# Splitting two float32 projections of the second attention into float32r parts, with in-place scans in a ring of three, batched small steps and a new order on every engine

## The chip, the cores and the metric

One NeuronCore of a Trainium2 chip runs the whole program. The metric is the device time of one execution in microseconds (us). The kernel before takes 1335.6 us (median of three runs, 1335.15 to 1338.34).

## What is computed

64 sequences of 128 tokens by 256 features (`x`) and as many of a context (`c`) go through four stages, all in float32 accuracy:

```
x1 = LN(attn16(relu(x Wq+bq), relu(c Wk+bk), relu(c Wv+bv), query mask) + x)   # 16 heads of 16
u  = rms(x1) @ in_proj; xBC = silu(causal_conv4(u)); dt = softplus(u_dt + bias)
y  = scan over 128 tokens: h = h*exp(dt*A) + dt*xh (x) B ; y = h.C + D*xh      # 8 heads of 64, state 128
h  = x1 + rms(y * silu(z)) @ out_proj
out = h + softmax((LN(h) Wq1)(c Wk1)^T / sqrt(32)) (c Wv1) @ Wo                # 8 heads of 32
```

The change is in the last line (the projections `Wq1` and `Wo`), in how the scan's decay tile is held, and in the order of everything.

## The kernel before, in words

The 64 sequences are worked on in 32 groups (`NG`) of two (`NB`), 256 tokens each. A group passes 25 kinds of step on TensorE (PE), 28 on VectorE (DVE), 29 on ScalarE (ACT), 15 on GpSimd (POOL) and 8 on the SyncE queue (SP). Each step is a small function of the group number `g` and a part; what an engine does is its list of calls, written out by hand: a prologue, a loop `for g in range(NG - 9)` in which the calls belong to up to six different groups, and an epilogue. All hand-offs are semaphores; every step waits for a count and raises one. An engine never leaves its list's order, so a step that waits holds all that stand behind it.

PSUM is eight banks. Which step writes which bank, and in which cyclic order, is the table `USES` (L21): an entry is (step, part, lag in groups) and its bank. `bank()` gives a step its bank and the semaphore of the step that used it last (`freed`), which must have been read out.

The steps that matter here, on PE:

- `proj3` (L315 to L321) multiplies in float32r with both operands split in a high and a low part: three matmuls (low x high, high x low, high x high) for each of the two halves of K=256. `q`, `k`, `k1`, `cp` (six parts) and `z` use it, `v`, `v1` and `o` have the same three products written out.
- `full` (L562 to L565), used by `q1`, and `wp` (L658 to L670) multiply in plain float32: two matmuls of 256 columns for a product where `proj3` has six. The trace shows each float32 matmul as two records.
- `sA`, `sT` and `sC` compute scores with 32-row pieces of the array, `av` and `oC` write 32-column pieces, `y` 64-column pieces. `tn`, `ot`, `nt`, `bd`, `bx`, `ht` and `tC` are transposes; `gm` and `dp` are small products.

On DVE: `mA` and `mC` are maxima of the scores, `tap` (18 a group) the convolution, `dc` (12 a group) the softplus polynomial, `scan` the decay products (L977, from `DB` into `L`), `lg` their product with `gm` (L986), `hm` (L1048) the mean term of the last LayerNorm, `fin` the last residual add, `nl` (L883) the low part of a split read from PSUM. On ACT, `he` copies the transposed LayerNorm output into `HT`, `oT` the attention output into `OT`. On POOL, `rs`, `nr` and `hr` raise variances to the power -1/2, one sequence at a time.

The decay goes through DRAM: `dk` (DVE) writes `decT`, `dec_out` (SP) stores it, `dec_in` (SP) loads it back broadcast to 128 partitions into `DB[b]`, and `scan` reads it. The two tiles `DB` are free again once the scan has read them.

The six stages overlap as follows in one turn of the loop: while PE does `cp(g+5)`, it also does `q(g+7)`, `sA(g+6)`, `y(g+4)`, `sC(g+3)` and `wp(g+2)`.

Of the kernel before, what the change touches and what calls it, by code (L numbers as in the profile page):

```python
# [5 lines left out]
F32 = mybir.dt.float32  # L6
# [30 lines left out]
def program(nc, a):  # L37
    with ExitStack() as ctx:
# [22 lines left out]
        wq1 = sb("wq1", [128, 2, 256])  # L61
        wo = sb("wo", [128, 2, 256])
# [33 lines left out]
        PTA = ring("PTA", 4, [128, 4, 128])  # L96
# [6 lines left out]
        sta = ring("sta", 4, [128, 48])  # L103
        stb = ring("stb", 4, [128, 16])
        stn = ring("stn", 4, [128, 1])
# [11 lines left out]
        DB = ring("DB", 2, [128, 1024])  # L117
        L = sb("L", [128, 8, 128])
        XH = sb("XH", [128, 512])
# [6 lines left out]
        HT = sb("HT", [128, 2, T])  # L126
# [89 lines left out]
        def sync(e):  # L216
# [97 lines left out]
        def tensor(e):  # L314
# [252 lines left out]
            def q1(g, m):  # L567
                if ok(g):
# [8 lines left out]
                    if m == 0:  # L577
                        e.wait_ge(s_h, 2 * g + 2)
# [1477 lines left out]
```

## Time and profile before

| | |
|---|---|
| median of 3 runs | 1335.6 us (1335.15 to 1338.34) |
| span of the profiled execution | 1337.2 us, 43414 instructions |
| the profiled execution's own time | no other number for it is given than the span, which lies inside the range of the runs, 1.6 us above their median |
| PE / PE weight loads / DVE / ACT / POOL busy | 1291.6 / 1148.0 / 1208.1 / 1130.8 / 928.7 us |
| granted TensorE clock | full (1.00) in the middle, 0.99 on average |
| DMA | 87.0 MB, 65 GB/s on average |

Busy time is the time in which an engine had an instruction in it. Durations of neighbouring instructions on one engine overlap a little in the records (by about 0.08 us on DVE), so the distance from one start to the next is what an instruction takes up of the engine. In the chain of waits ("the chain of work that ended last") each piece begins where the one before it ended, so its lengths do add up.

### The profile page before, as it was taken

Reading aid. Unit: us, or ns where it says so; the run is one execution under the profiler, and the core shown is the slowest. Engines: PE = TensorE matmul, PEld = TensorE weight load, DVE = VectorE, ACT = ScalarE, POOL = GpSimd, SP = SyncE. Lnnn points to the kernel's source line nnn. Section 1 sums busy time; section 2 is a strip of 40 time slices with the busy share of each in tenths; the row PEclk is TensorE's granted clock in tenths of the full one; section 3 lists DMA queues with packets and bytes.
Section 4 is the critical chain, followed back from the end, with each engine's and each line's share of the span. In section 5 each row is a group of like instructions: output and inputs, shape, how many; then the busy total and the mean of one; then the engine's idle time right before and its main releaser. Section 6 shows DMA issues by size and latency. Waiting matters only on the chain.

```text
span 1337.2 us, 43414 instructions
## 1 busy us (share of the span) xinstructions
PE 1291.6 (97%) x15624; PEld 1148.0 (86%) x15624; DVE 1208.1 (90%) x3056; ACT 1130.8 (85%) x3407; POOL 928.7 (69%) x1200
## 2 busy tenths in 40 slices
PE   5879999999999999999999999999999999999987
PEld 4668889988888998889998889989888898888875
DVE  6789999999999999999999999999999989999982
ACT  5658989888889988888988888998888898888875
POOL 3366777777767777777777776777777777766774
PEclk9889999999999999999999999999999999999999
DMA  6102221212221112222121222211222221111110
GB/s 203 40 34 72 69 77 38 70 56 69 77 77 62 52 49 69 77 77 77 38 66 60 69 77 77 61 53 50 69 77 77 71 71 34 62 56 57 49 57 25
DMA packets 41283, 87.00 MB, mean 65 GB/s; under 512 B 5744, under 2 KB 10992, under 8 KB 41072
## 3 DMA queue, kind: packets, MB, share of 16 engines
q1 hardware_dynamic: 40208, 83.81, 19.7%
q8 instruction: 127, 2.08, 0.6%
q14 instruction: 84, 0.69, 0.2%
q10 hardware_dynamic: 864, 0.42, 0.1%
HBM read 75.53 MB, written 8.68 MB: 63 GB/s over the span
## 4 chain that ended last, share of the span: by engine, by line
PE 87%; DVE 4%; ACT 4%; issue 2%; DMA 1%; POOL 1%; SPq 1%; ACTq 0%; DVEq 0%
PE bank L319 26%; PE bank L422 10%; PE bank L550 6%; PE bank L412 5%; PE bank L379 5%; PE bank L533 5%; PE bank L436 4%; PE bank L564 4%; PE bank L669 4%; PE bank L360 3%; PE bank L604 3%; PE bank L625 2%; PE bank L654 2%; PE bank L470 2%; PE bank L416 1%
## 5 line engine op out<-in xcount | busy, mean ns | idle before, releaser
L951 DVE SCALAR_TENSOR_TENSOR ACC<-bank,cw,ACC 128x250 f32<-128x250 f32 (+2 forms) x576 | 264.1, 462 | 5.9 <-ACT ACC L1535 3.3
L319 PE MATMUL bank<-xnT,wnl 128*128 128x256 f32 x640 | 201.6, 315 | 3.3 <-DVE xnL L883 2.3
L1622 ACT ACTIVATE PC<-bank,stc 128x128 f32<-128x128 f32 x512 | 182.5, 389 | 7.7 <-DVE stc L1068 4.3
L319 PE MATMUL bank<-xnL,wnh 128*128 128x256 f32 x640 | 180.3, 282 | 0.0
L319 PE MATMUL bank<-xnT,wnh 128*128 128x256 f32 x640 | 179.8, 281 | 0.0
L800 DVE TENSOR_REDUCE sta<-bank 128x4 f32<-128x512 f32 x256 | 163.7, 673 | 7.8 <-PE bank L379 7.5
L977 DVE TENSOR_TENSOR_SCAN L<-DB,id 128x1024 f32<-128x1024 f32 x64 | 146.8, 2293 | 0.8 <-DMA DB<-dec_scratch 0.8
L319 PEld LDWEIGHTS bank<-xnT,wnl 128*128 128x128 f32 x640 | 121.9, 190 | 26.0 <-issue 17.6
L1437 ACT ACTIVATE PTA<-bank 128x512 f32<-128x512 f32 x256 | 133.3, 628 | 9.0 <-PE bank L416 5.3
L1916 POOL TENSOR_TENSOR PC<-PC,stc 128x512 f32<-128x512 f32 x128 | 132.1, 1042 | 11.3 <-DVE stc L1075 11.3
L319 PEld LDWEIGHTS bank<-xnL,wnh 128*128 128x128 f32 x640 | 122.4, 191 | 0.0
L319 PEld LDWEIGHTS bank<-xnT,wnh 128*128 128x128 f32 x640 | 121.6, 190 | 0.0
L1871 POOL TENSOR_TENSOR XH<-XH,dtt 128x512 f32<-128x512 f32 x64 | 80.6, 1260 | 56.6 <-ACT XH L1552 56.5
L1622 ACT ACTIVATION_READ_ACCUMULATOR PC<-bank,stc 128x1 f32 x512 | 117.4, 229 | 0.0
L1535 ACT ACTIVATE ACC<-bank,cw 128x256 f32<-128x256 f32 x192 | 109.7, 573 | 8.3 <-PE bank L319 8.2
L1807 POOL TENSOR_TENSOR cL<-cT,cH 128x512 fp32r<-128x512 f32 x31 | 55.8, 1799 | 77.7 <-ACT cH L1372 77.7
L1880 POOL TENSOR_TENSOR Y<-Y,SZ 128x512 f32<-128x512 f32 x64 | 85.8, 1341 | 21.6 <-DVE Y L1011 18.9
L1886 POOL TENSOR_TENSOR Yl<-Y,Yh 128x512 fp32r<-128x512 f32 x64 | 82.6, 1291 | 20.0 <-ACT Yh L1580 19.9
L1423 ACT ACTIVATE NT<-bank,sel 128x128 fp32r<-128x128 f32 x256 | 73.4, 379 | 25.3 <-PE bank L392 25.3
L1636 ACT ACTIVATE PTC<-bank 128x512 f32<-128x512 f32 x128 | 78.6, 620 | 16.6 <-PE bank L422 16.3
L1068 DVE TENSOR_REDUCE stc<-bank 128x4 f32<-128x512 f32 x128 | 84.7, 683 | 7.5 <-PE bank L629 7.5
L1543 ACT ACTIVATE bank<-ACC 128x256 f32<-128x256 f32 x192 | 79.3, 415 | 8.5 <-DVE ACC L951 7.8
(210 smaller groups left out, 4709.9 us busy)
## 6 DMA issues: line engine op xcount, KB each, us to landing
DB<-dec_scratch SPq DMA_DIRECT2D x64, 512.0 KB, 4.0
cT<-in_cT SPq DMA_DIRECT2D x64, 256.0 KB, 2.6
xT<-in_xT SPq DMA_DIRECT2D x32, 256.0 KB, 4.0
xt<-in_xt SPq DMA_DIRECT2D x32, 256.0 KB, 3.8
out_x<-X SPq DMA_DIRECT2D x32, 256.0 KB, 4.0
QM<-qm_rows SPq DMA_DIRECT2D x32, 128.0 KB, 4.1
XC<-in_win SPq DMA_DIRECT2D x2, 644.0 KB, 6.7
PTC<-in_wout SPq DMA_DIRECT2D x2, 256.0 KB, 6.6
```

The source lines that it names most:

```text
L319: mm = e.matmul(t[:, c0:c0 + T], wt[:, k, m:m + 128], x[:, k, :], start=(n == 0), stop=(n == 5))
L422: mm = e.transpose(t[:, c0 + i * 128:c0 + (i + 1) * 128], src(i), ident[:, :])
L800: e.tensor_reduce(sta[ns % 4][:, 4 * j:4 * j + 4], t[:, :].rearrange("p (i k) -> p i k", i=4), AX_X, ALU.max, negate=True).then_inc(s_mA, 1)
L951: e.scalar_tensor_tensor(out=w, in0=t[:, 0:T].rearrange("p (b t) -> p b t", b=NB)[:, :, 0:125 + k], scalar=cw[:, c, k:k + 1], in1=w, op0=A ...
L977: e.tensor_tensor_scan(L[:, :, :].rearrange("p h t -> p (h t)"), DB[b][:, :], id8[:, :, :].rearrange("p h t -> p (h t)"), 0.0, ALU.mult, A ...
L1068: e.tensor_reduce(stc[g % 4][:, 4 * i:4 * i + 4], t[:, :].rearrange("p (i k) -> p i k", i=4), AX_X, ALU.max, negate=True).then_inc(s_mC, 1)
L1437: e.activation(PTA[n % 4][:, :, :], t[:, :].rearrange("p (i k) -> p i k", i=4), ACT.Exp).then_inc(s_eA, 1)
L1535: e.activation(ACC[n % 3][:, :, :], t[:, 0:T].rearrange("p (b t) -> p b t", b=NB), ACT.Identity, bias=cw[:, c, 4:5], scale=cw[:, c, 3:4]). ...
L1622: op = e.activation(PC[n % 4][:, p, :], t[:, p * 128:(p + 1) * 128], ACT.Exp, bias=stc[g % 4][:, 4 * i + p:4 * i + p + 1], accum_out=stc[g ...
L1880: e.tensor_tensor(cv(Y[:, :]), cv(Y[:, :]), SZ[:, :, b * 128:(b + 1) * 128], ALU.mult).then_inc(s_ga, 1)
L1886: e.tensor_tensor(Yl[:, :], Y[:, :], Yh[:, :].bitcast(F32), ALU.subtract).then_inc(s_yl, 1)
L1916: e.tensor_tensor(PC[n % 4][:, :, :], PC[n % 4][:, :, :], stc[g % 4][:, 16 + 4 * i:20 + 4 * i].unsqueeze(2).to_broadcast([128, 4, 128]), A ...
```

## The change

1. **Two projections in float32r.** `q1` and `wp` use three float32r matmuls for each float32 one. Their weights are split at the start (`wq1h`/`wq1l`, `woh`/`wol`). Their inputs need a low part as well, so `he` now writes `HTh` and a new DVE step `hl` (two a group, 128x256, PSUM and SBUF in) writes `HTl`; `oT` writes `OTh` and a new DVE step `ol` (one a group, 128x512) writes `OTl`. The banks `ht` and `oC` are freed by the new steps.
2. **Scan in place.** `L` is gone. `scan` and `lg` write into the tile they read, `DB`, now a ring of three over the 64 sequences. `dec_in` waits until `y` of three sequences before has read the tile.
3. **Buffers.** `XH` is a ring of two instead of one tile, `PTA` a ring of six instead of four; `sta`, `stb`, `stn` are views of tiles that hold both sequences of a group.
4. **Batched steps.** `rs`, `nr`, `hr` on POOL and `hm` on DVE run once for a group on 128x2 values instead of twice on 128x1.
5. **Order.** Prologues and epilogues are gone; each engine has one loop over `g` from -5 (SP from -6) to `NG - 1`, and `if ok(g)` in each step leaves out what doesn't exist. The order in the loop and the table `USES` are new.
6. `dynamic_dma_scratch_size=1024` is given to the program's constructor.

```diff
-        wq1 = sb("wq1", [128, 2, 256])
-        wo = sb("wo", [128, 2, 256])
+        wq1h, wq1l = (sb(n, [128, 2, 256], F32R) for n in ("wq1h", "wq1l"))
+        woh, wol = (sb(n, [128, 2, 256], F32R) for n in ("woh", "wol"))
-        PTA = ring("PTA", 4, [128, 4, 128])
+        PTA = ring("PTA", 6, [128, 4, 128])
-        DB = ring("DB", 2, [128, 1024])
-        L = sb("L", [128, 8, 128])
-        XH = sb("XH", [128, 512])
+        DB = ring("DB", 3, [128, 1024])
+        XH = ring("XH", 2, [128, 512])
...
             def dec_in(g, b):
-                    if ns >= 2:
-                        e.wait_ge(s_l, ns - 1)
-                    e.dma_start(DB[b][:, :], scratch[g, b * 1024:(b + 1) * 1024].rearrange(
+                    if ns >= 3:
+                        e.wait_ge(s_y, ns - 2)
+                    e.dma_start(DB[ns % 3][:, :], scratch[g, b * 1024:(b + 1) * 1024].rearrange(
...
             def q1(g, m):
-                        e.wait_ge(s_h, 2 * g + 2)
-                    full(t, 0, wq1, m, HT).then_inc(s_1p, 1)
+                        e.wait_ge(s_hl, 2 * g + 2)
+                    proj3(t, 0, wq1h, m * 128, HTh, HTl, wq1l).then_inc(s_1p, 1)
...
             def wp(g, i):
-                    e.wait_ge(s_oT, g + 1)
+                    e.wait_ge(s_ol, g + 1)
                     for b in range(NB):
+                        n = 0
                         for kk in range(2):
-                            mm = e.matmul(t[:, b * 256:(b + 1) * 256], OT[:, 2 * b + kk, :], wo[:, kk, :],
-                                          start=(kk == 0), stop=(kk == 1))
+                            for x, w in ((OTh, wol), (OTl, woh), (OTh, woh)):
+                                mm = e.matmul(t[:, b * 256:(b + 1) * 256], x[:, 2 * b + kk, :], w[:, kk, :],
+                                              start=(n == 0), stop=(n == 5))
+                                n += 1
...
+            def hl(g, b):
+                    e.tensor_tensor(HTl[:, :, c], t[:, 0:256].rearrange("p (k t) -> p k t", k=2),
+                                    HTh[:, :, c].bitcast(F32), ALU.subtract).then_inc(s_hl, 1)
...
+            def ol(g):
+                    e.tensor_tensor(OTl[:, :, :], t[:, :].rearrange("p (k t) -> p k t", k=4), OTh[:, :, :].bitcast(F32),
+                                    ALU.subtract).then_inc(s_ol, 1)
```

The new loop on PE, in its order (`g` left out: `q+5` is `q(g+5)`, a second number is the part):

```
tC.0 sT+3.1 sA+4.0 q+5.0 av+3.4-7 bx+2.0 gm+2.0 tC.1 ot+3.1 ht+1.0 q+5.1 ht+1.1 tC.2 sA+4.1 y+2.0
k+5.0 k1+1.1 q1+1.0 v+5 q1+1.1 tC.3 nt+3 bx+2.1 sC+1 oC.0 oC.1 gm+2.1 cp+3.0 dp+3 cp+3.1 y+2.1 wp
cp+3.2 o+2.0 cp+3.3 v1+1 tn+4.0 z+3.0 cp+3.4 o+2.1 bd+3 sT+4.0 cp+3.5 tn+4.1 z+3.1 av+4.0-3
k1+2.0 k+5.1 ot+4.0
```

The parts of the new DVE loop that the prediction speaks of:

```
... scan+2.1 nl+3 mC+1.0 mC+1.1 lg+2.1 mC+1.2 ol mC+1.3 ... dk+3 tap r1 xc tap tap hs hh tap xc tap tap hg hs hg xc sz
rc+4.0 kk1+2.0 xo+4.0 hm+2 scan+3.0 mA+5.0-3 lg+3.0 rc+4.1 rC xo+4.1 bs hl+2.0 hl+2.1 ...
```

And the new SP loop:

```
dec_in(g+2,0) load_x(g+6) load_u(g+2) dec_in(g+2,1) dec_out(g+3) store(g) load_t(g+4) load_m(g+6) load_c(g+6)
```

## Rows read from the trace of the kernel before

**Rows 1.** The page's head and its line of busy times.
```profile
span 1337.2 us, 43414 instructions
PE 1291.6 (97%) x15624; PEld 1148.0 (86%) x15624; DVE 1208.1 (90%) x3056; ACT 1130.8 (85%) x3407; POOL 928.7 (69%) x1200
```

**Rows 2.** Busy time by stretch: us; PE, PEld, DVE, ACT, POOL; clock, DMA, GB/s.
```profile
49.82:166.62 116.80, 106.80 (x1228) 92.76 (x1226) 108.18 (x267) 88.52 (x245) 67.64 (x90) 0.94 0.19 62
166.62:1195.59 1028.97, 1028.25 (x12691) 921.97 (x12690) 958.06 (x2444) 908.49 (x2756) 752.47 (x962) 1.00 0.21 65
641.65:681.13 39.48, 39.48 (x491) 35.40 (x489) 36.73 (x96) 34.90 (x108) 28.81 (x38) 1.00 0.21 65
1195.59:1232.65 37.06, 36.08 (x451) 30.82 (x451) 35.58 (x93) 30.72 (x95) 23.84 (x35) 1.00 0.15 52
1232.65:1269.30 36.65, 35.00 (x400) 30.23 (x400) 33.73 (x89) 31.73 (x101) 26.39 (x34) 1.00 0.15 45
1269.30:1337.20 67.90, 54.15 (x539) 45.98 (x538) 40.09 (x99) 44.14 (x155) 39.82 (x46) 0.97 0.12 40
```

**Rows 3.** The chain of waits, 600 to 680 us: start, us, piece.
```profile
603.99 0.91 PE bank L319 x6
...
607.96 1.42 PE bank L604 x12
609.37 0.71 PE bank L319 x6
610.08 1.73 PE bank L669 x8
...
617.22 1.01 PE bank L436 x32
...
621.48 1.10 PE bank L412 x32
622.58 0.24 PE bank L416 x4
622.82 0.59 PE bank L422 x4
...
624.11 0.44 PE bank L422 x4
...
625.65 1.08 PE bank L379 x16
...
631.25 0.87 PE bank L564 x4
632.12 1.07 PE bank L379 x16
```

**Rows 4.** DVE groups by shape, 602 to 997 us: count, busy, mean ns, idle before.
```profile
L883 DVE TENSOR_TENSOR xnL<-bank,xnT 128x256 fp32r<-128x256 f32 x20 | 7.6, 420 | 0.6
L1011 DVE TENSOR_TENSOR Y<-bank,DX 128x512 f32<-128x512 f32 x20 | 13.7, 685 | 2.6 <-PE bank L533 2.6
L1048 DVE SCALAR_TENSOR_TENSOR stb<-stb 128x1 f32<-128x1 f32 x20 | 11.8, 589 | 0.0
```

**Rows 5.** Instructions on the tile stb: the line of L1048.
```profile
L1048 DVE SCALAR_TENSOR_TENSOR stb<-stb x64: 127/499/1002, 106.6 to 1312.3; 128x1 f32<-128x1 f32 x64
```

**Rows 6.** DVE and SP in order of time, 641 to 682 us: start, us.
```profile
656.10 0.28 DVE L939 COPY decT<-bank 16x127 f32<-16x127 f32 x1 [0.28 <-PE bank L481]
...
664.82 2.28 DVE L977 TENSOR_TENSOR_SCAN L<-DB,id 128x1024 f32<-128x1024 f32 x1
667.02 0.67 DVE L800 TENSOR_REDUCE sta<-bank 128x4 f32<-128x512 f32 x1
...
670.17 0.42 DVE L847 BATCH_NORM_STATS2 sta<-xa 128x6 f32<-128x256 f32 x1
...
658.94 0.33 SPq L280 DMA_DIRECT2D DB<-dec_scratch  x1
```

**Rows 7.** The page's DMA issues: KB each, us from issue to landing.
```profile
DB<-dec_scratch SPq DMA_DIRECT2D x64, 512.0 KB, 4.0
```

More of the change, by code:

```diff
@@ L102, in program @@
         X2 = ring("X2", 5, [128, NB, D])
-        sta = ring("sta", 4, [128, 48])
-        stb = ring("stb", 4, [128, 16])
-        stn = ring("stn", 4, [128, 1])
+        STA = ring("STA", 2, [128, NB, 48])
+        sta = [STA[n // NB][:, n % NB, :] for n in range(4)]
+        STB = ring("STB", 2, [128, NB, 16])
+        stb = [STB[n // NB][:, n % NB, :] for n in range(4)]
+        STN = ring("STN", 2, [128, NB, 1])
+        stn = [STN[n // NB][:, n % NB, :] for n in range(4)]
         stc = ring("stc", 4, [128, 32])
@@ L134, in program @@
         d_xT, d_cT, d_cU, d_xt = (sem(n) for n in ("d_xT", "d_cT", "d_cU", "d_xt"))
-        d_scr, d_db, d_out = ([sem(f"{n}{i}") for i in range(2)] for n in ("d_scr", "d_db", "d_out"))
+        d_scr, d_out = ([sem(f"{n}{i}") for i in range(2)] for n in ("d_scr", "d_out"))
+        d_db = [sem(f"d_db{i}") for i in range(3)]
         z_ones, z_pad, z_wo2, z_wol, z_cw, z_wq1, z_ea, z_bq, z_neg, z_v, z_split = (
@@ L560, in ht @@
                     turn(t, lambda i: xh[b][:, i * 128:(i + 1) * 128], 0, 2).then_inc(s_ht, 1)
-            def full(t, c0, w, m, x):
-                for k in range(2):
-                    mm = e.matmul(t[:, c0:c0 + T], w[:, k, m * 128:(m + 1) * 128], x[:, k, :], start=(k == 0), stop=(k == 1))
-                return mm
             def q1(g, m):
@@ L788, in tensor @@
-            oC(NG - 1, 1); wp(NG - 1, 0)
+            for g in range(-5, NG):
+                tC(g, 0)
+                sT(g + 3, 1)
+                sA(g + 4, 0)
+                q(g + 5, 0)
+                av(g + 3, 4)
+                av(g + 3, 5)
+                av(g + 3, 6)
+                av(g + 3, 7)
+                bx(g + 2, 0)
+                gm(g + 2, 0)
+                tC(g, 1)
+                ot(g + 3, 1)
+                ht(g + 1, 0)
+                q(g + 5, 1)
+                ht(g + 1, 1)
+                tC(g, 2)
+                sA(g + 4, 1)
+                y(g + 2, 0)
+                k(g + 5, 0)
+                k1(g + 1, 1)
+                q1(g + 1, 0)
+                v(g + 5, 0)
+                q1(g + 1, 1)
+                tC(g, 3)
+                nt(g + 3, 0)
+                bx(g + 2, 1)
+                sC(g + 1, 0)
+                oC(g, 0)
+                oC(g, 1)
+                gm(g + 2, 1)
+                cp(g + 3, 0)
+                dp(g + 3, 0)
+                cp(g + 3, 1)
+                y(g + 2, 1)
+                wp(g, 0)
+                cp(g + 3, 2)
+                o(g + 2, 0)
+                cp(g + 3, 3)
+                v1(g + 1, 0)
+                tn(g + 4, 0)
+                z(g + 3, 0)
+                cp(g + 3, 4)
+                o(g + 2, 1)
+                bd(g + 3, 0)
+                sT(g + 4, 0)
+                cp(g + 3, 5)
+                tn(g + 4, 1)
+                z(g + 3, 1)
+                av(g + 4, 0)
+                av(g + 4, 1)
+                av(g + 4, 2)
+                av(g + 4, 3)
+                k1(g + 2, 0)
+                k(g + 5, 1)
+                ot(g + 4, 0)
@@ L1015, in r1 @@
                     ns = 2 * g + b
+                    if ns == 0:
+                        e.wait_ge(z_wq1, 2)
+                        for k in range(2):
+                            e.scalar_tensor_tensor(out=wq1l[:, k, :], in0=wq1u[:, k, :], scalar=pc[:, 10 + k:11 + k],
+                                                   in1=wq1h[:, k, :].bitcast(F32), op0=ALU.mult, op1=ALU.subtract).then_inc(z_q1l, 1)
                     t, _ = bank("o", b, g)
@@ L1987, in gpsimd @@
-            lo_u(NG - 1); r2(NG - 1, 1); hr(NG - 1, 0); hr(NG - 1, 1); nC(NG - 2, 2); nC(NG - 2, 3); nC(NG - 1, 0)
-            nC(NG - 1, 1); nC(NG - 1, 2); nC(NG - 1, 3)
+            for g in range(-5, NG):
+                nC(g, 2)
+                dx(g + 2, 0)
+                qm(g + 4, 1)
+                lo_x(g + 5)
+                hr(g + 1)
+                xr(g + 3, 0)
+                qm(g + 5, 0)
+                lo_c(g + 5)
+                xd(g + 2, 0)
+                xr(g + 3, 1)
+                nC(g, 3)
+                rs(g + 3)
+                nr(g + 3)
+                ga(g + 2, 0)
+                dx(g + 2, 1)
+                s2_(g + 2, 0)
+                xd(g + 2, 1)
+                yl(g + 2, 0)
+                nC(g + 1, 0)
+                ga(g + 2, 1)
+                r2(g + 2, 0)
+                s2_(g + 2, 1)
+                yl(g + 2, 1)
+                nC(g + 1, 1)
+                lo_u(g + 2)
+                r2(g + 2, 1)
```

841 lines of the change are left out of this document (245 added, 596 removed), and 22 rows, old and new, of the table USES.

## The prediction
> **What bounds the kernel now.** I read the busy times first [rows 1], then the busy times by stretch [rows 2], then the chain of waits in the middle [rows 3]. The page gives PE 97% of the span, DVE 90%. By stretch this becomes sharp: I cut the span at the starts of `dp`, which comes once in each group. From 166.62 to 1195.59 us lie 26 groups, 1028.97 us, 39.58 us each; PE is busy for 1028.25 of them. One turn (641.65 to 681.13) takes 39.48 us: PE busy in all of it, DVE in 36.73, ACT in 34.90, POOL in 28.81. The chain there is nothing but PE pieces that follow each other without a gap. So the middle costs what PE's list costs, and DVE is next, 2.75 us behind. The ends are different: the three groups up to 166.62 (116.80 us) and the last two turns (37.06 and 36.65) have PE and DVE both partly idle, and behind the last `dp` come 67.90 us in which a chain across all engines sets the time.
>
> Is a busy PE a bound? The rows say yes, because its pieces are laid start to start: a `proj3` of six matmuls takes 0.71 us wherever it stands behind a full-array product [rows 3]. The Trainium skill (Perfetto Trace Analysis, Identifying the Most-Contended Engine) holds matmul busy time for a bad measure and wants the busy share of the weight loads instead. By that rule PE has 35.40 of 39.48 us in the turn, less than DVE's 36.73, and DVE would be the engine to look at; that is the third case below.
>
> **The change on PE.** `q1` is two pieces of 0.87 us a group (L564 x4), `wp` one of 1.73 (L669 x8) [rows 3]. In the new kernel `q1` is two `proj3`, the same shape as the 0.71 us piece (L319 x6), and `wp` has the shape of `v1`, 12 matmuls in 1.42 us (L604 x12). That is 2 x 0.87 - 2 x 0.71 = 0.32 and 1.73 - 1.42 = 0.31, together 0.63 us less in each group. The matmul count rises, their time falls.
>
> The order changes one more price. A full-array piece directly behind a row- or column-tiled one is longer: `proj3` 0.91 instead of 0.71 behind `y` (603.99), four transposes 0.59 instead of 0.44 behind `sT` (622.82 against 624.11) [rows 3]. The old order has seven such places (`cp` behind `oC`, `y` and `sT`, `v` behind `y`, `tn` behind `av`, `tC` behind `sT`, `ht` behind `sA`): 4 x 0.20 + 3 x 0.15 = 1.25 us. The new one has seven too (`q` behind `sA`, `bx` behind `av`, `k` behind `y`, `gm` behind `oC`, `wp` behind `y`, `cp` behind `sT`, `k1` behind `av`): 5 x 0.20 + 2 x 0.15 = 1.30. I take no difference. Between two tiled kinds nothing is lost: `sA` takes 1.08 us behind `av` and 1.07 behind the full-array `q1` (625.65, 632.12). The Trainium skill (TensorEngine Tiling (Array Packing), Key Properties) says that each change of tiling mode drains the engine; by that the new order, which has two tiled-to-tiled changes where the old has three, would gain one more drain, some 0.15 us a group or 4 us in all. The two `sA` rows speak against it, and the sum leaves it out.
>
> PE alone would therefore turn in 39.48 - 0.63 = 38.85 us.
>
> **The change on DVE.** Added: `hl` twice, like `nl` (L883, 0.42 us, the same shape and operands), and `ol` once, like L1011 (0.685 us, 128x512 out of a bank) [rows 4]. Neighbours overlap by 0.08, so they take up 0.34, 0.34 and 0.60: 1.28 us. Removed: one of two `hm`, 0.59 on average, 0.51 taken up. Its length runs from 0.127 to 1.002 us for the same 128 values [rows 5], so it mostly waits for something. The Trainium skill (SBUF — State Buffer, on the shared port pair) says that a DVE instruction with two SBUF inputs is held up by a GpSimd instruction that reads SBUF; the spread agrees. The new `hm` may cost from 0.05 to 0.9. Net +0.77 us, between +0.4 and +1.2. DVE then has 36.73 + 0.77 = 37.50 busy of a 38.85 us turn: 1.35 us of slack where it had 2.75. Scan and `lg` in place are the same instructions on other addresses: nothing, between -0.1 and +0.1 each.
>
> **What stays at nothing, and under which cover.** `he` and `oT` only change the name of their output. POOL has 10.7 idle us in the turn [rows 2] and loses three pairs of small steps; waiting for both sequences costs the first a little of its lead. Startup splits `Wo` and `Wq1` (one ACT copy, one POOL and two DVE subtractions, under 3 us together on three engines) beside a stretch (49.82 to 166.62) with over 8 idle us on each [rows 2]. The 1 KB scratch: every DMA in the kernel is issued from SP or ACT, none from POOL; I take nothing, and have no row that bounds it but the 4.0 us to landing of the decay tile [rows 7]. `PTA`'s six tiles and `XH`'s two take waits away that the middle of PE doesn't show.
>
> **Where the new order is tight.** I laid the new lists end to end, with the durations of these rows. Two loops across engines come out close to their limit.
> (a) `ot+4.0` (PE's last step) releases `rc` on DVE, which is followed by `kk1`, `xo`, `hm`, `scan` and four `mA`; the last `mA` frees bank 4 for `ot+3.1`. On DVE the scan takes up 2.20 us (664.82 to 667.02), four `mA` with `kk1`, `rc` and `xo` 3.15 (667.02 to 670.17), `hm` 0.5 [rows 6]: 5.85 and two hand-offs. On PE the steps between are `tC` 0.44, `sT` 1.34, `sA` 1.07, `q` 0.91, `av` 1.01, `bx` 0.59, `gm` 0.11, `tC` 0.44: 5.91 us [rows 3] (`gm` is one transpose of four). If a hand-off costs 0.1 to 0.2, PE loses 0.1 to 0.4 us a turn; if `hm` is short, nothing. Between 0 and 0.4 I take 0.05, as the two sums differ by less than one hand-off and `hm` may well be short.
> (b) `dk` to `scan` goes through DRAM. Before, `dec_in` was issued 2.84 us after `dk` began (656.10, 658.94) and landed 4.0 later [rows 6, 7]: 6.84 us, where DVE reached the scan after 8.72. In the new list 7.0 us of DVE work lie between them, so the tile lands just in time; ahead of it on SP stand `store`, `load_t`, `load_m` and `load_c(g+6)`, which waits for POOL's `lo_u(g+2)`. DVE's slack covers 1 us of lateness. I take 0, between 0 and 1 us a turn.
>
> **The ends.** Head: up to the 26 turns only the first `q1` run; -0.3, between -0.6 and +2 for the plain loop. Tail, behind 1195.59: four groups' `q1` and six `wp` would give 10 x 0.31 = -3.1 if PE set the time; if DVE does, `hl` four times 0.68, `ol` six times 0.60, less `hm` four times 0.51, add 4.3. In between, with the chain of the last group longer by one `hl` and one `ol`: +1.0, between -3 and +4.5. That the hand-made prologue and epilogue go may add some us; the clipped loops keep nearly the same sequence of calls, so I add nothing and widen the range by 3 to either side.
>
> **Sum.** 26 x (-0.63 + 0.05) = -15.1; head -0.3; tail +1.0: -14.4 us. Against the profiled 1337.2 that is 1322.8, against the median, 1.6 lower, 1321.2 us. Case one's own range: 26 x 0.35 = 9 us worse to 26 x 0.05 better, with the ends, 1312 to 1333.
>
> **Rivals.**
> 1. *PE stays the bound, PE's saving arrives* (0.68): 1321 us. For it: PE without a gap for 1000 us, shapes with their own rows.
> 2. *The new order loses less than the old at the ends, or also saves a drain per turn* (0.12): -4 to -8 more, 1313 to 1317.
> 3. *DVE becomes the bound* (0.13), the rule on weight loads taken seriously. DVE's turn is 37.50 plus the waits it can't fill. Of today's 2.75 idle us some are only PE's lead. With half of them left, 1.4, the turn is 38.9 and case one holds; with 1.9 it is 39.4, and the tail's +4.3 is whole: 26 x -0.08 + 4.3, some 1338.
> 4. *Slower: `scan` waits for its decay tile, loop (b)* (0.07). The place is the wait of `scan` on `d_db`; the price is the lateness beyond DVE's slack of 1.35 us. It decides from 2.0 us of lateness on (1.35 + 0.63): at 3 us, which `load_c` would bring if `lo_u` on POOL comes that late, each turn is 38.85 + 1.65 = 40.5, 26 x 1.0 = +26 and 1366; at 2.2 it is 1342. Against it: POOL's slack.
> That the change doesn't do what it says (float32r no faster) has no chance worth a number: the shapes stand beside each other in the trace.
>
> **Numbers.** The likeliest case gives 1321. Range 1310 to 1337: it holds cases one and two and the near half of three. What a measurement can tell from no change is 0.3%, 4 us. Faster than 1331.6: nearly all of one and two, a third of three, 0.84. Same: 0.09. Slower than 1339.6: 0.07.
>
> **What would show it.** PE busy near 1270 us, the turn at 38.8 to 39.0 between starts of `dp`, L564's and L669's successors at 0.71 and 1.42 a piece. DVE busy about 37.5 in a turn, with `hl` at 0.42 and `ol` near 0.69. Loop (a) right: a PE wait at `ot` released by `mA`, 0.05 to 0.4 a turn. Loop (b) right: DVE waits at `scan` for the DMA of `DB`. Wrong: PE gaps of over 0.5 us in each turn, with DVE without any; or a tail behind the last `dp` far from 68 us.

## The result, and the profile after

The changed kernel is slower: 1374.74 us median of 4 runs (1370.19 to 1376.79) beside 1335.72 of the kernel before in the same session, ratio 1.028, 95% interval 1.026 to 1.030. The forecast was 1321. The profiled execution took 1374.97 us with a span of 1373.2, so the spans stand against each other: 1337.2 [rows 1] and 1373.2, 36.0 us more. One run of the kernel below with SP's old order (1778.6 us) and one of the third kernel with the scan moved (1477.4 us) fell in a slower state of the chip, and the medians here leave them out; the 1354.8 us that later expectations name is the first kernel's median with it.

The page's head and line of busy times of the changed kernel:

```profile
span 1373.2 us, 43866 instructions
PE 1284.6 (94%) x15880; PEld 1156.7 (84%) x15880; DVE 1227.5 (89%) x3122; ACT 1132.7 (82%) x3408; POOL 915.3 (67%) x1009
```

TensorE does 7.0 us less work than before and is idle 43 us more. To see where, I cut both spans at the start of the third and of the thirtieth `dp`. Busy time by stretch of the kernel before (us; PE, PEld, DVE, ACT, POOL; clock, DMA, GB/s), for these cuts:

```profile
0.00:126.80 126.80, 98.87 (x1064) 83.92 (x1064) 101.95 (x238) 79.54 (x194) 56.01 (x87) 0.91 0.28 92
126.80:1195.40 1068.60, 1067.30 (x13178) 956.87 (x13175) 996.60 (x2540) 944.52 (x2866) 782.48 (x1002) 1.00 0.21 65
1195.40:1337.20 141.80, 125.42 (x1389) 107.22 (x1387) 109.59 (x279) 106.78 (x349) 90.24 (x113) 0.99 0.14 44
```

The same three stretches of the changed kernel, then two single turns of its middle and the stretch between its first two `dp`:

```profile
0.00:138.70 138.70, 101.92 (x1074) 87.79 (x1074) 97.48 (x244) 80.80 (x196) 58.12 (x76) 0.86 0.25 82
138.70:1217.30 1078.60, 1053.76 (x13382) 955.34 (x13381) 1016.92 (x2592) 945.54 (x2867) 768.05 (x839) 1.00 0.19 64
1217.30:1373.20 155.90, 128.88 (x1429) 113.53 (x1427) 113.11 (x288) 106.40 (x349) 89.13 (x95) 0.92 0.12 40
...
456.50:495.30 38.80, 38.80 (x498) 35.34 (x497) 37.55 (x97) 34.92 (x108) 30.13 (x32) 1.00 0.20 67
656.70:697.10 40.40, 38.99 (x498) 35.34 (x497) 37.48 (x97) 35.09 (x107) 28.27 (x32) 1.00 0.19 64
...
56.20:98.40 42.20, 32.31 (x317) 28.01 (x317) 35.12 (x88) 25.06 (x62) 17.20 (x17) 0.78 0.16 54
```

The head is 11.9 us longer, the 27 turns of the middle 10.0 (39.95 for 39.58 us each), the end 14.1. The turn of 38.80 us is what the forecast had for every turn (38.85): TensorE busy throughout, VectorE 37.55. Where the turn of 40.40 us differs is one wait. VectorE around the first scan of the group, in the short turn and in the long one (start, us, instruction, in brackets the idle time before it):

```profile
476.13 0.26 DVE L760 RECIPROCAL STA<-bank 128x16 f32<-128x16 f32 x1 [0.63 <-PE bank L415]
...
477.05 2.29 DVE L907 TENSOR_TENSOR_SCAN DB<-DB,id 128x1024 f32<-128x1024 f32 x1
...
676.34 0.26 DVE L760 RECIPROCAL STA<-bank 128x16 f32<-128x16 f32 x1 [0.63 <-PE bank L415]
...
678.86 2.29 DVE L907 TENSOR_TENSOR_SCAN DB<-DB,id 128x1024 f32<-128x1024 f32 x1 [1.58 <-DMA DB<-dec_scratch]
681.07 2.46 DVE L732 TENSOR_REDUCE STA<-bank 128x4 f32<-128x512 f32 x4
```

From `rc` (L760) to the scan it takes 0.92 us in the one and 2.52 in the other, 1.60 more; the turns differ by 1.68 from start to start of `dp` (38.80 and 40.48; the stretches above are cut to a tenth). Behind the scan stand the four `mA` (L732), and TensorE waits for them. Its waits in the long turn, all of them:

```profile
681.79 0.65 PE L415 MATMUL bank<-ident,XC 128*128 128x128 f32 x4 [0.94 <-DVE STA L732]
683.58 0.66 PE L415 MATMUL bank<-ident,OA 128*128 128x128 f32 x4 [0.48 <-DVE STA L732]
```

SP's queue in this turn:

```profile
670.13 0.32 SPq L277 DMA_DIRECT2D dec_scratch<-decT  x1
670.50 0.42 SPq L291 DMA_DIRECT2D out_x<-X  x1
670.97 0.43 SPq L258 DMA_DIRECT2D xt<-in_xt  x1
671.44 0.46 SPq L271 DMA_DIRECT2D QM<-qm_rows  x1
672.00 0.38 SPq L240 DMA_DIRECT2D cT<-in_cT  x1
672.47 0.38 SPq L285 DMA_DIRECT2D DB<-dec_scratch  x1
```

The decay load is issued 2.6 us behind `dk` (669.83 to 672.47), sooner than before (2.84), but behind four other transfers, and it is there only 6.4 us later. Before, only the mask and x were issued close by, and behind it. Over the whole kernel the loads of decay tiles take 3.4 to 7.7 us, median 4.7 where it was 4.0 [rows 7]. That median mixes the two loads of a group. The first one, which stands behind the four transfers, went from 3.8 us (3.5 to 6.3) to 5.0 (4.3 to 7.7); the second went from 4.6 to 3.7. From the list of waits:

```profile
DVE DB L907 <- DMA DB<-dec_scratch: 27.0, 25, 3.2
PE bank L415 <- DVE STA L732: 26.2, 43, 2.8
```

(us in all, times, longest.) Before, the first of these was 0.8 us in all. 27 turns of 38.80 us are 1047.6; the middle is 31.0 us longer than that.

A tile that is late by very little costs more than its lateness. GpSimd's `xr` (L1616) becomes ready at almost the same time as the first scan. Here are both, in the short turn of above and in the next one, which takes 39.56 us:

```profile
477.13 2.75 POOL L1616 TENSOR_TENSOR xa<-xa,xt 128x256 f32<-128x256 f32 x1 [0.98 <-DVE xa L770]
...
515.94 0.74 POOL L1616 TENSOR_TENSOR xa<-xa,xt 128x256 f32<-128x256 f32 x1 [1.11 <-DVE xa L770]
515.97 2.85 DVE L907 TENSOR_TENSOR_SCAN DB<-DB,id 128x1024 f32<-128x1024 f32 x1
```

In the short turn the scan (477.05) starts first and takes 2.29 us, and `xr` is the long one. In the next turn the scan is 0.1 us later, `xr` starts first, and the scan takes 2.85 us. The 27 turns of the middle fall into three kinds. In 3 the scan starts first: 38.80 to 39.11 us. In 9 it is late by 0.1 to 0.55 us, takes 2.41 to 2.87 us, and the turn takes 39.50 to 39.62, some 0.75 more whatever the lateness. In 15 it is late by 0.88 to 3.15 us and finds `xr` done; it takes 2.29 us, and the turn is longer than 38.80 by the wait and 0.0 to 0.2 us.

### The profile page after: what moved, and what is told of

Read it like the earlier page. It is cut to its first block and busy times, and to the rows that moved or that the text cites. A ratio compares the mean times of both kernels' runs of the same rounds, so it can differ in the third digit from the quotient of the medians.

```text
span 1373.2 us, 43866 instructions
## 1 busy us (share of the span) xinstructions
PE 1284.6 (94%) x15880; PEld 1156.7 (84%) x15880; DVE 1227.5 (89%) x3122; ACT 1132.7 (82%) x3408; POOL 915.3 (67%) x1009
## 5 line engine op out<-in xcount | busy, mean ns | idle before, releaser
L883 DVE SCALAR_TENSOR_TENSOR ACC<-bank,cw,ACC 128x250 f32<-128x250 f32 (+2 forms) x576 | 271.3, 471 | 6.5 <-ACT ACC L1390 1.7
L907 DVE TENSOR_TENSOR_SCAN DB<-DB,id 128x1024 f32<-128x1024 f32 x64 | 161.8, 2528 | 27.2 <-DMA DB<-dec_scratch 27.0
L732 DVE TENSOR_REDUCE STA<-bank 128x4 f32<-128x512 f32 x256 | 162.8, 677 | 10.1 <-PE bank L372 10.1
L1641 POOL TENSOR_TENSOR DX<-XC,pc 128x512 f32<-128x512 f32 x64 | 128.2, 2003 | 17.0 <-DVE XC L896 17.0
L1480 ACT ACTIVATION_READ_ACCUMULATOR PC<-bank,stc 128x1 f32 x512 | 131.0, 256 | 0.0
L1390 ACT ACTIVATE ACC<-bank,cw 128x256 f32<-128x256 f32 x192 | 119.1, 620 | 10.7 <-PE bank L312 10.7
L1600 POOL TENSOR_TENSOR QT<-QT,QM 128x256 f32<-128x256 f32 x64 | 50.3, 787 | 90.4 <-ACT QT L1245 79.9
L1315 ACT ACTIVATE junk<-X 128x256 uint8<-128x256 f32 x64 | 26.7, 417 | 92.3 <-DVE X L801 89.8
L1616 POOL TENSOR_TENSOR xa<-xa,xt 128x256 f32<-128x256 f32 x64 | 54.7, 855 | 68.2 <-DVE xa L770 68.0
L1659 POOL TENSOR_TENSOR Y<-Y,SZ 128x512 f32<-128x512 f32 x64 | 82.4, 1287 | 7.3 <-DVE Y L941 7.2
```

Of the source, the lines that this page charges most:

```text
L732: e.tensor_reduce(sta[ns % 4][:, 4 * j:4 * j + 4], t[:, :].rearrange("p (i k) -> p i k", i=4), AX_X, ALU.max, negate=True).then_inc(s_mA, 1)
L883: e.scalar_tensor_tensor(out=w, in0=t[:, 0:T].rearrange("p (b t) -> p b t", b=NB)[:, :, 0:125 + k], scalar=cw[:, c, k:k + 1], in1=w, op0=A ...
L907: e.tensor_tensor_scan(DB[ns % 3][:, :], DB[ns % 3][:, :], id8[:, :, :].rearrange("p h t -> p (h t)"), 0.0, ALU.mult, ALU.add).then_inc(s_ ...
L1390: e.activation(ACC[n % 3][:, :, :], t[:, 0:T].rearrange("p (b t) -> p b t", b=NB), ACT.Identity, bias=cw[:, c, 4:5], scale=cw[:, c, 3:4]). ...
L1480: op = e.activation(PC[n % 4][:, p, :], t[:, p * 128:(p + 1) * 128], ACT.Exp, bias=stc[g % 4][:, 4 * i + p:4 * i + p + 1], accum_out=stc[g ...
L1641: e.tensor_tensor(cv(DX[:, :]), XC[g % 2][:, 0:4, b * 128:(b + 1) * 128], pc[:, 14:18].unsqueeze(2).to_broadcast([128, 4, 128]), ALU.mult) ...
```

## The experiments

Eighteen kernels ran. All times are medians; the stretches of a run are cut as above, at the third and the thirtieth `dp`: head, middle, end.

**The decay load alone.** Theory after reading the trace: the loop through the decay tile. One line of SP's loop moves:

```
-                dec_in(g + 2, 0)
                 load_x(g + 6)
 ...
                 dec_out(g + 3)
+                dec_in(g + 3, 0)
                 store(g)
```

> After, with one line of SP's loop moved: the load of the decay tile for part 0 of a group is issued right behind the decay's store, ahead of the output store and the loads of xt, mask and c (1.9 us of issue, and four bulk transfers that share the DMA engines with it). Theory A (loop b: the first scan waits for its decay tile, 25 waits of 3.2 us on average in the after profile, and its lateness goes through mA, the banks and ot into every turn): the waits of scan for the decay load shrink from 27.0 us in sum to under 5, the turn goes from 40.0 us to 39.0 to 39.4, the time from 1374.7 to about 1350 (1345 to 1358). Rival B (the turn is set by bank 4: rc, kk1, xo, hm, scan and four mA between two ot's, so by VectorE's work): the waits for the load go, VectorE waits elsewhere instead, the time changes by under 5 us. Rival C (the loss is in the head and the end alone): no change of the turn, under 3 us.

Measured: 1383.64 us, 9 us slower. The waits of the scan for its tile are gone from the middle, all of them, and others stand in their place. From this kernel's list of waits:

```profile
ACT cH L1227 <- DMA cT<-in_cT: 48.5, 30, 4.1
POOL xa L1616 <- DMA xt<-in_xt: 42.0, 22, 2.9
```

The decay load waits on SP for the decay store to land, and c and xt queue behind it. (My "3.2 us on average" was wrong: 3.2 is the longest, the mean is 1.1.) None of the three cases was right. But the sizes say what sets the turn: the middle (1094.1 us) is 46.5 us over 27 turns of 38.80, and ScalarE's wait for c in it adds up to 44.6. In the four turns from 426 to 582 us, where these waits were 0.5 to 0.6 us, the turns were 39.1 to 39.2 us.

**SP's order as before.** So it is the place of every load on that queue, not of one. The changed kernel with SP's old loop, from group 0 on:

```
+            for g in range(NG):
+                load_c(g + 6)
+                dec_out(g + 3)
+                dec_in(g + 3, 0)
+                load_m(g + 6)
+                load_x(g + 7)
+                load_u(g + 3)
+                dec_in(g + 3, 1)
+                load_t(g + 5)
+                store(g)
```

> After, with SP's loop in the order of the kernel before (load c, decay store, decay load 0, mask, x, u, decay load 1, xt, output store), from group 0 on; nothing else. Where the decay load alone was moved up, the turns were 39.1 us in the stretch 464 to 582 us and 40.5 to 42 us elsewhere, and there ScalarE waited 2 us a turn for cT and GpSimd 2 us for xt: the loads queued on SP behind the decay load, which waits for the decay store to land. Theory A (the loop runs through SP's queue: each load waits for its place, the decay tile or c and xt, and no order is good that has c or xt just behind the decay's store and load): c ahead of the store and xt far behind it give turns of 39.0 to 39.3 us, the time falls by 20 to 27 us to about 1350. Rival B (the uneven turns come from another place, the port that VectorE and GpSimd share or the banks): the turns stay at 40 us in the mean, the time within 5 us of 1374.7.

Measured: 1353.32 us (median of 1346.01, 1353.32 and 1356.35), 21 below the change, ratio to the kernel before 1.0107 (1.0067 to 1.0147) for 1.028. The profiled execution is the fastest of the three (span 1344.2), so its stretches show some 7 us less than the median would. By stretch:

```profile
0.00:135.90 135.90, 100.49 (x1075) 86.90 (x1075) 97.48 (x244) 80.67 (x196) 60.20 (x76) 0.89 0.26 84
135.90:1192.30 1056.40, 1049.69 (x13382) 954.61 (x13381) 1016.29 (x2592) 942.73 (x2867) 794.94 (x839) 1.00 0.21 66
1192.30:1344.20 151.90, 122.75 (x1429) 107.75 (x1427) 112.55 (x288) 106.40 (x349) 89.20 (x95) 0.98 0.12 40
```

The middle falls by 22.2 us, to 39.13 us a turn, and is now 12.2 us shorter than before the change. The scan's waits in it are 4.1 us for 25.3, the decay load's median landing 3.7 us. The head gives 2.8 us, the end 4.0. This run settles the largest term. The engines' orders and instructions are the same in both kernels, so what the middle gained belongs to SP's list alone. It is 22 us in this execution and 18 to 20 in those of three later kernels with the same list and small edits besides (middles of 1058.5 to 1060.6 us). The gain comes as fewer late scans: in 17 of the 27 turns the scan now takes its 2.29 us on time (38.72 to 39.07 us a turn), in 8 it is just behind `xr` (39.47 to 39.57), and in 2 it waits longer.

The other way round, the kernel before with the changed kernel's SP loop:

> The kernel before, with the changed kernel's loop on SP (decay load 0, x, u, decay load 1, decay store, output store, xt, mask, c, from group -6 on) in place of its own, and nothing else. Theory A (SP's order is the cause of the longer turn): turns of 40 us for 39.5 and more, the time 1350 to 1370. Rival B (the loss lies in the orders of the other engines, and before's scan, which runs later in its turn, bears this order): 1336 to 1342.

Measured: 1353.80 us, 17 above the kernel before. By stretch the profiled execution is 3.5 us longer in the head, 5.8 in the middle (39.79 us a turn) and 5.1 at the end. Of the middle's 5.8 some 4 lie in its last turn alone (43.4 us, with a wait of 2.0 at a transpose and a granted clock of 0.96 in it); the other 26 take 39.65 us for 39.58. So the time is theory A's and the steady turn is not: there the old orders bear the queue almost for nothing, since the scan had nearly two microseconds to spare (6.84 against 8.72 in the forecast), though the first load's median landing is 5.0 us here too. At both ends they lose, and there SP's hand-written prologue and epilogue went as well, so that loss isn't the order's alone.

**GpSimd's subtractions in the head.** `if ns == 1` becomes `if ns == 3` in `xr`.

> After, with GpSimd's three weight subtractions (3.9 us, at 40.0 to 43.8 us of the profile) moved from its xr(0,1) to its xr(1,1), one group later. Theory A (TensorE's idle 8.0 us before the first dp is the wait for xn(0,1), and GpSimd's subtractions stand ahead of the xa that leads to it): the first dp starts 3 to 4 us earlier, at about 52.5 us, and the time falls by 3 to 4 us, to about 1371. Rival B (the head waits for the statistics that are now made for both sequences at once): the first dp starts within 1 us of 56.2 and the time stays.

Measured: 1379.91 us, and the first `dp` at 51.5 for 56.2 us. At the third `dp` 2.8 of the 4.7 us are left, and the middle is 6.7 us longer, with 33.4 us of waits for the decay tile for 25.3. With SP's old order as well:

> The same, with GpSimd's weight subtractions one group later as well (in the kernel with that change alone the first dp started 4.7 us earlier, 51.5 for 56.2 us, and the time did not fall, its turns being 40.2 us in the mean). Theory A (the head's gain was lost again in uneven turns and stays once the turns are even): 3 to 5 us below the run before, about 1346. Rival B (the head's gain is taken back by what comes next whatever the turns are): the same time as the run before.

Measured: 1351.77 us; third `dp` at 133.0 for 135.9. So the head gains 3 us in the profiles; the medians differ by 1.6, which the spread of these runs (5 and 10 us) doesn't tell from nothing.

**The split taken out of the new orders.** q1 and wp in plain float32, no `hl`, no `ol`:

```
-                    proj3(t, 0, wq1h, m * 128, HTh, HTl, wq1l).then_inc(s_1p, 1)
+                    for k in range(2):
+                        mm = e.matmul(t[:, 0:T], wq1h[:, k, m * 128:(m + 1) * 128], HTh[:, k, :], ...)
+                    mm.then_inc(s_1p, 1)
```

> After, with the orders, rings and scratch as they are, but the second Q and output projection in plain float32 again: no low parts of HT, OT, wq1 and wo, no hl and ol on VectorE. Per turn TensorE gets 0.63 us more (39.5 busy), VectorE 1.28 us less (36.2). Theory A (the turn of 40.0 us is set by the decay loop and VectorE's path between two ot's, not by TensorE's work): the time stays within 8 us of after's, or falls by up to 15, since hl no longer stands ahead of the mA's. Rival B (the split is what costs, by the tiled to full changes or by hl and ol): it falls by 20 us or more, to before's 1336. Rival C (TensorE is the bound): it rises by 15 to 20 us.

Measured: 1400.84 us, 26 above the change. Rival C was nearest. TensorE's busy time in the 27 turns is 1071.8 us for 1053.8, 0.67 a group, where the forecast had 0.63; the rest is waits for the decay tile again (37.2 us in the middle for 25.3). On TensorE the split is worth what it was said to be, in these orders.

**The split put into the old orders.** `hl(g+4)` ahead of `bs(g+6,1)`, `ol(g+2)` behind `yd(g+4,1)`:

> Before, with its own orders on all engines, and the float32r split of the two projections alone: hl(g+4) ahead of bs(g+6,1), ol(g+2) behind yd(g+4,1) on VectorE, the one swap q1 with sA on TensorE, DMA scratch 1024 bytes; no ring of three, no scan in place. Theory A (the split itself is a gain of 0.63 us of TensorE per turn, 32 turns, less what hl and ol push late, and the loss of the change is in its new orders): 1320 to 1332, faster than before by 4 to 15 us. Rival B (the split itself costs: VectorE's 1.28 us more per turn stand in the way of the next mA's and TensorE waits for them): 1336 to 1370.

Measured: 1434.95 us, 97 above the kernel before and outside both ranges. The turns are all 42.6 us, with three waits of TensorE in each:

```profile
598.32 0.39 PE L551 MATMUL bank<-woutl,Yh 128*128 128x256 f32 x1 [1.00 <-DVE OTl L1096]
624.43 0.38 PE L320 MATMUL bank<-cH,wkl 128*128 128x256 f32 x1 [1.22 <-DVE HTl L1061]
626.77 1.15 PE L380 MATMUL bank<-KT,QT 32*128 32x256 f32 x16 [0.73 <-ACT PTC L1664]
```

A bank is free only once its low part is taken, so the next user of the bank waits, and that is another step (`o`, `k`), not q1 or wp. With the low parts earlier:

```
+                hl(g + 4, 0)
                 mA(g + 7, 2)
                 mA(g + 7, 3)
-                hl(g + 4, 0)
                 hl(g + 4, 1)
 ...
+                ol(g + 2)
                 tap(g + 5, 1)
                 yd(g + 4, 1)
-                ol(g + 2)
```

> The kernel before with its orders and the split alone, as in the run of 1435 us, whose turns were 42.6 us at 39.66 us of TensorE busy: TensorE waited 1.22 us for hl(g+4,0) at the k projection that takes its bank, 1.00 us for ol(g+2) at o, 0.73 us for a mask of ScalarE at sA. Here hl(g+4,0) stands two mA earlier, ol(g+2) ahead of the tap and yd, and q1 ahead of sA again. Theory A (the split costs nothing but these three waits, each due to where its low part stands): turns of 39.0 to 39.6 us, the time 1318 to 1340. Rival B (VectorE's added 1.28 us a turn come back as other waits): turns over 40 us, 1350 or more.

Measured: 1365.87 us. In the quiet middle the turn is 39.6 and TensorE is busy in 79.97 of 80 us: neither theory's number for the time, A's for the turn. Taken from start to start over two turns, wp falls from 3.44 to 2.86 us and q1 from 3.65 to 3.32, but the k, q and input projections that come behind hand-offs rise (k's first products 1.09 to 1.32, q's last 0.95 to 1.29), so nothing is left. Of the 29 us over the kernel before, 3 lie in the head, 15 at the end and most of the rest in the turns next to them, where the low parts kept their first places. The output projection's split alone:

> The kernel before, its orders on all engines, with the split of the output projection alone (no split of Q): ol(g+2) ahead of the tap and of yd, DMA scratch 1024 bytes. TensorE's time for wp fell from 1.72 to 1.43 us a turn in the run with both splits and early low parts, and its k and q projections behind hl rose instead, so that its turn was 39.6. Theory A (the output projection's part is a gain by itself, the Q part is eaten by hl): turns of 39.2 us, 1326 to 1334, faster than both kernels. Rival B (VectorE's 0.6 us more a turn comes back in small waits of TensorE): turns of 39.5 us or more, 1336 to 1345.

Measured: 1342.67 us, ratio 1.0029 (1.0019 to 1.0039). Ten turns of the middle take 394.10 us for 395.30, 0.12 a turn gained where wp's products gained 0.29. The end is 148.1 us for 141.8, and there TensorE waits twice for `ol` in front of wp (4.2 us). The time is rival B's, the turn lies between the two theories; in all it is a loss at the limit of what can be told.

**The scan behind the mA's.**

```
-                scan(g + 3, 0)
                 mA(g + 5, 0)
                 mA(g + 5, 1)
                 mA(g + 5, 2)
                 mA(g + 5, 3)
+                scan(g + 3, 0)
                 lg(g + 3, 0)
```

> After, with VectorE's scan(g+3,0) moved behind the four mA that it stands ahead of: the first scan of a group asks for its decay tile 2.5 us later and no longer stands between rc and the mA's on which TensorE's next turns wait. SP's order stays as in the change. Theory A (two loops meet in that scan: late decay tile, and rc to mA; both are 2.3 to 4 us too tight): the wait of scan for the load falls from 27 us in sum to under 8, TensorE's waits at its turns for mA from 26 us to under 5, the turn from 40.0 to 38.9 us, the time to about 1342 to 1350. Rival B (SP's order costs by other ways, c and xt above all): the turn stays near 40 us, 1362 to 1376.

> Both: SP's loop in the order of the kernel before, and scan(g+3,0) behind the four mA. With SP's order alone the turns were 39.2 us in the mean, 38.8 in the good ones, the rest of the wait being at rc and at scan. Theory A: 38.8 us in every turn, 10 to 14 us below the run with SP's order alone (1354.8), about 1342. Rival B (TensorE's own work, not VectorE's path, makes the 39.2): no change, 1350 to 1356. Head and end keep their 9 and 4 us above the kernel before.

> The same, and the head thinned: GpSimd's three weight subtractions stand ahead of its first dx, where it waits 17 us, and VectorE's four subtractions of woutl (1.66 us) stand behind the first yd instead of ahead of it; with scan behind the mA's the building of the masks (3.9 us, in the first scan) no longer stands ahead of them either. Theory A: TensorE's waits of 4.6, 2.8 and 4.8 us in the first 90 us shrink by 6 to 10 us together, the time is 6 to 8 us below the run before: about 1334, level with the kernel before or a little faster. Rival B (the head is bound by the first loads and by the statistics made for both sequences at once): within 2 us of the run before.

Measured: 1444.61, 1445.80 and 1449.90 us. All expectations fell, and in the same way. The waits for the decay tile are gone; from the timeline of the second of the three:

```profile
593.70 3.38 DVE L921 TENSOR_TENSOR_SCAN DB<-DB,id 128x1024 f32<-128x1024 f32 x1
597.19 1.22 DVE L930 TENSOR_TENSOR DB<-DB,bank 128x1024 f32<-128x1024 f32 x1
...
598.47 0.66 PE L429 MATMUL bank<-ident,PC 128*128 128x128 f32 x4 [2.58 <-DVE DB L930]
```

`lg` (L930) reads the bank of `gm`, which the turn `tC(g,2)` takes over; `lg` comes 2.5 us late and TensorE waits 2.58. The scan has no free side: ahead of it stands the tile, behind it mA's banks, and with it `lg`'s.

**The scratch alone**, in the kernel before:

> The kernel before with a DMA scratch of 1024 bytes and nothing else. Theory: no change, 1335.7 within 2 us. Rival (the small scratch is what makes the loads late): 1345 or more, with the decay load's landing over 4.5 us for 4.0.

Measured: 1338.00 us for 1338.25, ratio 0.9998 (0.9987 to 1.0009). Nothing.

**VectorE's way from `rc` to the mA's.** `kk1(g+2,0)` ahead of `rc(g+4,0)`, `hm(g+2)` behind the four `mA`; with SP's old order, with that and a thinner head, and with SP's new order:

> After with SP's loop in the order of the kernel before, and on VectorE kk1(g+2,0) ahead of rc(g+4,0), where VectorE waits 0.6 us for TensorE's turn, and hm behind the four mA: the way from rc to the last mA is 0.4 us shorter, and nothing of it is late for lg (in the run with scan behind the mA's lg came 2.5 us late, and TensorE waited 2.6 us a turn for the bank of gm at its tC turn). Theory A (of the 0.4 us a turn that SP's order leaves over 38.8, the rest is this way, with waits of 0.48 us at ot(.,1) in one turn in two or three): 38.8 to 39.0 us in the mean for 39.2, the time 5 to 12 us below the 1354.8 of SP's order alone. Rival B (the rest is decay loads that are late now and then): 39.2 again, no change.

> The same with the head thinned: GpSimd's three weight subtractions ahead of its first dx (it waits 17 us there), VectorE's four subtractions of woutl behind the first yd, the building of the masks behind the first lg instead of ahead of the first scan. Theory A: TensorE's waits of 4.6, 2.8 and 4.8 us in the first 90 us shrink by 6 to 10 us together and the second dp starts at about 88 us for 94 to 98: 6 to 8 us below the run before, about 1336 to 1342. Rival B (the head is bound by its first loads and by the statistics that are made for both sequences at once): within 2 us of the run before.

> After with SP's order as the change has it, and kk1 and hm moved as in the run before the last. It tells whether VectorE's way between two turns alone carries a part of the loss. Theory A (the decay load, late by 3 us, hides what is taken off ahead of it: scan starts when the load lands): no change, 1370 to 1376. Rival B (VectorE's way is a loop by itself): 1358 to 1366.

Measured: 1408.59, 1408.29 and 1431.80 us. The turns of the first are 41 us, and the cause is `hm`, an instruction on two columns. ScalarE and TensorE in that kernel's trace:

```profile
614.58 0.60 ACT L1348 ACTIVATE xh<-X,STB 128x256 f32<-128x256 f32 x1 [2.50 <-DVE STB L996]
615.08 0.58 ACT L1315 ACTIVATE OA<-bank 128x512 f32<-128x512 f32 x1
...
615.80 0.63 PE L429 MATMUL bank<-ident,OA 128*128 128x128 f32 x4 [2.22 <-ACT OA L1315]
```

`xh` needs `hm` (L996), `oa` stands behind `xh` on ScalarE, and TensorE's `ot` behind `oa`. These runs tell of `hm` and nothing of `kk1`. With `hm` back in its place:

> After with SP's loop in the order of the kernel before, and kk1(g+2,0) ahead of rc(g+4,0) on VectorE, in the 0.6 us that VectorE waits there; hm stays ahead of the scan, since in the two runs with hm behind the four mA ScalarE waited 2.5 us for it at xh, with oa queued behind, and TensorE 2.2 us a turn for ot's bank. Theory A (VectorE's way from rc to the last mA makes the last 0.4 us of a turn): 38.8 to 39.0 us in the mean for 39.2, 5 to 12 us below the 1354.8 of SP's order alone. Rival B (the rest is decay loads that are late now and then): 39.2 us, no change.

> The same with the head thinned: GpSimd's three weight subtractions ahead of its first dx, the building of the masks in the 4.1 us that VectorE waits at its first nl, the four subtractions of woutl ahead of the wait of the first scan. Theory A: 6 to 8 us below the run before, about 1335 to 1340, level with the kernel before. Rival B (the head is bound by its first loads and by the statistics that are made for both sequences at once): within 2 us of the run before.

Measured: 1350.58 and 1347.35 us. The first has turns of 39.28 us, no shorter than the 39.13 of SP's order alone, and 8.7 us of waits for the decay tile in the middle for 4.1. Rival B: the rest of the turn is late loads. In 13 of its 27 turns the scan starts ahead of `xr`, and they take 38.78 us on average; 9 with a scan late by 0.1 to 0.5 us take 39.52, and 5 with a longer wait 40.17. The 3 us between the medians are within the spread of these runs. In the second the third `dp` comes at 131.8 us for 134.9, and the time is 3.2 us lower: half of what theory A gave. It is the fastest version of the whole change, ratio 1.0074 (1.0057 to 1.0091). I found none that beats the kernel before.

## Why the prediction was wrong

**TensorE's work: right.** 0.63 us a group less was forecast, 0.67 measured between the kernels with and without the split; the turn was to be 38.85 us, and an undisturbed one takes 38.80. q1 gained more (1.82 to 1.38 us, from start to start; one of the old pieces takes 0.96 that way, not 0.87) and wp less (1.72 to 1.47 or 1.52). No run separates the drains of the two orders. TensorE's busy time of the whole kernel was to be near 1270 us and is 1284.6: the middle has 13.5 us less for the 17.0 that 27 turns promise, and the head and the end have 6.5 more, at a lower granted clock (0.86 for 0.91, 0.92 for 0.99).

**VectorE's work: right.** 37.55 us busy in a turn for 37.50; `hl` 0.415 and `ol` 0.681 us. `hm` took 0.15 us in the turns above and 1.08 where it stood behind the mA's, so it does mostly wait. VectorE did not become the bound (rival 3): in the 38.80 us turn it has 1.25 us to spare.

**Loop (a): right for itself.** 0.05 us a turn was taken, and the turns in which the scan is on time show nothing. All others have a wait of 0.48 at `ot(.,1)`, also where the tile is only 0.1 us late. What the sum of durations couldn't show is that GpSimd's `xr` stands right beside the scan: the loop has a reserve of about 0.1 us, and behind it a step of 0.75.

**Loop (b): this is the step that failed.** Three things in it. The landing was taken as the old 4.0 us although I had listed what would now stand ahead of it on SP; I looked there only for a wait (`load_c` for `lo_u`, which does not occur), not for what four transfers do to the fifth. The first load, the one behind the four, lands after 4.3 to 7.7 us, median 5.0. Second, "DVE's slack covers 1 us of lateness" was the wrong cover: VectorE's idle time lies elsewhere in the turn, and here the scan stands inside loop (a), which has none. So a lateness of 0.1 to 0.55 us costs 0.75 us of turn, and from 0.9 us on each us is a us of turn (1.58 of wait, 1.68 of turn above); nothing is free up to 2.0 us, as rival 4 had it. Third, the two loops were summed as if they were apart. The same table of waits gives the price: 25.3 us of waits for the decay tile and 2.6 for c in the middle, and the middle is 31.0 us over 27 turns of 38.80. Rival 4 (0.07) named the place, and its 1366 for 3 us of lateness was the nearest number, by luck: the delay that it named doesn't occur, and the mean over the 25 late tiles is 1.1 us. That SP's list is the cause of most of the middle's loss is shown by the exchange in the new kernel (21 us off the median, 18 to 22 off the middle). The exchange in the old kernel costs 17 us, but nearly all of it at and near the ends, so it doesn't show a price per turn. That transfers issued just ahead share the DMA engines with the decay load is how I read the landings. It was not measured alone, and why the landing differs between turns with the same issue times (a tile asked for at 472.30 is there by 477.05, one asked for at 672.47 only at 678.86) stays open. The DMA records give one hint. In the six kernels that have this list on SP, 26 of the 160 first loads of the middle have a 16 KB packet of the queue that the page calls `q8 instruction` 1.0 to 3.6 us behind their issue. They take 6.2 us (median, 5.5 to 8.1) where the other 134 take 5.1, and in the changed kernel they are the four slowest. No run was made to test it.

**The ends: this failed too.** -0.3 was taken for the head and +1.0 for the tail, 3 us either way for the plain loop; the head cost 11.9 us and the end, with its last two full turns, 14.1. Of the head 2.8 are SP's order and about 3 the three placements of setup work in the kernel of 1347.35 us (subtractions, masks, woutl); some 5 to 6 are open, among them what the steps now made for both sequences at once may cost, which no run tested. TensorE's longest idle time there, 7.99 us ahead of the first `xn`, waited for a chain through GpSimd that has three weight subtractions of 1.3 us in it. Of the end 4.0 are SP's order and 10.1 are left with it undone. I put them down to the plain loop, whose last turn is 42.1 us (with SP's old order) where the hand-written end had 36.0; no run gave the new orders a hand-written end. Behind the last `dp` come 74.9 us for 68.5, the sign that the forecast had named. (The last cut of [rows 2], 1269.30, lies 0.6 us behind the start of that `dp`.) The split has no share in it in these orders (without it the end is 156.8 us for 155.9), though the output projection's split alone cost 6.3 us there in the old ones. "The clipped loops keep nearly the same sequence of calls" was the sentence that was wrong: they keep the order of the full loop, in which setup and drain work have no place of their own.

**The scratch: right**, nothing.

With SP's old order the sum nearly works out in the middle: in its fastest run that is 12.2 us shorter than before, where the forecast's 0.58 a turn makes 15.7 for these 27. The change has a gain in it and loses it three times, some 20 us in the middle by one queue's order, and at both ends.

## What to carry to other kernels

When one loop per engine replaces hand-written lists, the DMA queue's list is an engine's list too: write down for each load what it waits for, what waits behind it, and how much is issued just ahead of a small load that a loop depends on. An engine's idle time in a turn covers a delay only if it lies behind the delayed step and ahead of the next hand-off; if the step stands in another tight loop, there is no cover, and if another engine's instruction can slip in ahead of it, a tenth of a microsecond of lateness can cost seven. And price the first and last groups by themselves, since a loop that is right in the middle can cost ten us at either end.

## What the runs showed that I had not expected

- Moving one small instruction on VectorE (`hm`, 0.15 us) behind the scan and four `mA` makes TensorE wait 2.2 us in every turn, by way of ScalarE's in-order queue; moving the scan behind the four makes it wait 2.6, by way of a bank.
- The scan takes 2.53 us on average (2.28 to 3.15) where it took 2.29 before. In one turn the long one (651.61, 2.67 us) lies beside GpSimd's `dx` (652.09, 3.02 us, 1.04 at its shortest). The Trainium skill (SBUF — State Buffer, on the shared port pair) says that the two engines lock each other out there, and both rows fit; over the kernel it is 15 us of VectorE's time. For the first scan of a group the turns above separate it, some 0.75 us each time that `xr` starts first; the second scan takes 2.6 to 2.7 us in nearly every turn, also in those of 38.80.
- The granted clock at the end was 0.92 in the changed kernel and 0.98 with SP's old order, and the same 1429 matmuls were busy 128.9 and 122.8 us. TensorE was idle more in the first; which of the two is the cause was not tried.
- The new kernels scatter more from run to run than the kernel before: 1345.6 to 1354.4 us in six runs of one of them, which agrees with a turn whose length depends on when a load lands.
